# A cross-attention kernel whose inputs come laid out by columns, with column maxima for the scales and double-buffered fp16 parts

## The reference

```
q, k_t, v_t  = heads(x @ W_q), heads(text @ W_k), heads(text @ W_v)
probs_t      = softmax(q k_t^T / 4)                       # per head, 508 text tokens
text_out     = probs_t @ v_t
k_ip, v_ip   = heads(ip @ W_k_ip), heads(ip @ W_v_ip)     # 4 image tokens
qsem         = l2norm(probs_t @ text)                     # per head, 512 features
sem          = qsem @ l2norm(ip)^T
probs_ip     = softmax(q k_ip^T / 4 + 0.5 * sem) * spatial_mask
out          = (text_out + probs_ip @ v_ip) @ W_out + b_out + x
```

## Time and profile before

| | us |
|---|---|
| median of the runs | 1828.28 (1827.54 to 1833.78, 3 runs) |
| the profiled execution, as timed | 1832.93 |
| its span, first to last instruction | 1831.2 |
| busy over the span: PE, DVE, ACT, POOL | 1742.6, 1244.5, 1184.2, 1231.0 |
| first product of the first stage | at 31.94 |
| last mirror transpose of the first stage ends | at 336.78 |
| first exponential of the second stage | at 357.98 |
| first unit | at 371.65 |

### The profile page before, as it was taken

One profiled execution on the slowest core, in us unless ns is written; L12 is line 12 of the kernel. 1 busy time (PEld: TensorE's weight loads), 2 busy tenths in 40 slices (PEclk: granted clock), 3 DMA queues, 4 the chain that ended last, 5 costly groups with the idle time before them and its releaser, 6 DMA issues.

```text
span 1831.2 us, 48590 instructions
## 1 busy us (share of the span) xinstructions
PE 1742.6 (95%) x14421; PEld 1106.2 (60%) x14421; DVE 1244.5 (68%) x2872; ACT 1184.2 (65%) x2644; POOL 1231.0 (67%) x1414
## 2 busy tenths in 40 slices
PE   4999999499999999999999999999999999999899
PEld 2767766356666566666566666656566666666455
DVE  5445454267777677777677777767677777777684
ACT  3444555367777677777677777767677777777321
POOL 3122112278888788888788888878788888888310
PEclk8899999799999999999999999999999999999999
DMA  5354553736777777765665686666657656854133
GB/s 160 109 144 134 137 171 106 142 72 91 91 100 112 89 93 100 113 91 91 104 91 89 101 117 92 101 93 102 86 85 115 91 89 100 99 90 77 38 101 100
DMA packets 427592, 187.95 MB, mean 103 GB/s; under 512 B 384728, under 2 KB 415072, under 8 KB 427392
## 3 DMA queue, kind: packets, MB, share of 16 engines
q1 hardware_dynamic: 425088, 183.40, 59.0%
q10 hardware_dynamic: 2304, 2.14, 0.4%
HBM read 67.21 MB, written 34.39 MB: 55 GB/s over the span
## 4 chain that ended last, share of the span: by engine, by line
POOL 39%; PE 27%; issue 24%; DMA 3%; DVE 3%; POOLq 2%; ACT 1%; SPq 1%; ACTq 0%; DVEq 0%
POOL probs L587 17%; POOL probs L594 17%; PE bank L1287 13%; PE bank L1495 3%; PE bank L1430 3%; POOL reduced L602 2%; POOL wkv L580 2%; PE bank L1431 2%; DMA late<-wkv 2%; PE bank L1345 2%; PE bank L1496 1%; POOL reduced L601 1%; PE bank L1395 1%; PE bank L1404 1%; DVE reduced L1018 1%
## 5 line engine op out<-in xcount | busy, mean ns | idle before, releaser
L1430 PE MATMUL bank<-u_sb,late 127*128 127x508 f16 x2560 | 946.2, 376 | 0.0
L1431 PE MATMUL bank<-u_sb,late 127*128 127x508 f16 (+3 forms) x2560 | 763.0, 298 | 0.0
L1091 DVE TENSOR_REDUCE neg_max<-bank 128x1 f32<-128x508 f32 x640 | 439.1, 686 | 368.5 <-PE bank L1395 368.4
L580 POOL TENSOR_TENSOR wkv<-probs,wkv 128x508 f16<-128x508 f32 x320 | 358.6, 1121 | 219.6 <-ACT wkv L817 219.4
L1429 PE MATMUL bank<-v_ring,late 127*128 127x41 f16 x2560 | 468.8, 183 | 12.5 <-DMA late<-wkv 8.0
L1100 DVE SCALAR_TENSOR_TENSOR probs<-bank,probs 128x508 f32<-128x508 f32 x640 | 432.5, 676 | 6.3 <-PE bank L1431 6.3
L1429 PEld LDWEIGHTS bank<-v_ring,late 127*128 127x128 f16 x2560 | 247.2, 97 | 245.6 <-DMA late<-wkv 10.7
L594 POOL TENSOR_TENSOR probs<-probs,late 128x508 f32<-128x508 f32 x320 | 368.6, 1152 | 0.0
L587 POOL TENSOR_TENSOR probs<-probs,wkv 128x508 f32<-128x508 f32 x320 | 357.6, 1118 | 0.0
L1430 PEld LDWEIGHTS bank<-u_sb,late 127*128 127x128 f16 x2560 | 248.3, 97 | 167.5 <-issue 2.4
L1395 PE MATMUL bank<-x_sb,work 96*128 96x508 bf16 x640 | 242.1, 379 | 41.7 <-DMA x_sb<-k_parts 18.5
(11 more groups left out here) (166 smaller groups left out, 1804.7 us busy)
## 6 DMA issues: line engine op xcount, KB each, us to landing
x_sb<-in_x SPq DMA_DIRECT2D x16, 640.0 KB, 5.1
reduced<-in_ctx SPq DMA_DIRECT2D x32, 256.0 KB, 5.0
work<-q_parts SPq DMA_DIRECT2D x32, 240.0 KB
x_sb<-k_parts SPq DMA_DIRECT2D x32, 238.1 KB
u_parts<-u_sb SPq DMA_DIRECT2D x8, 825.5 KB, 4.2
u_sb<-u_parts SPq DMA_DIRECT2D x8, 825.5 KB, 5.3
v_parts<-v_sb SPq DMA_DIRECT2D x8, 820.0 KB, 8.2
v_ring<-v_parts SPq DMA_DIRECT2D x32, 205.0 KB, 9.0
```

Source lines behind the costliest of these rows:

```text
L580: nc.gpsimd.tensor_tensor(rows[:, 1, :, 0:TP], probs[:, j % PROB_RING, :].rearrange("p (k t) -> p k t", k=TT), rows[:, 0, :, 0:TP], ALU.su ...
L1091: nc.vector.tensor_reduce(neg_max[:, j % 4:j % 4 + 1], bank[S_BANK + j % 2][:, 0:T], AX.X, ALU.max, negate=True)\
L1430: nc.tensor.matmul(y, hi_k, u_sb[0:TP, par, GH[k]:GH[k] + T], start=(k == 0), stop=False)
L1431: done = nc.tensor.matmul(y[:, k * TP:T], hi_k, u_sb[0:TP, par, UL[k]:UL[k] + U_COLS[k]], start=False, stop=(k == TT - 1))
```

## The change

The host hands over x and the text by columns (`x_cols`, `ctx_cols`), the image tokens apart, and the weight of Q with its last 64 rows twice. PE's 28 transposes of inputs per batch go. One ACT instruction for x and one for the text write the high parts, two and one of DVE the rest, into `x_t[par]` and `ctx_t[par]`, of which there are two now, by the parity of the batch. The inputs of the batch after the next are loaded into one raw buffer (`raw`) as soon as the next one's parts are written.

x's last 64 features: the high part lies in partitions 0 to 63 of the third tile and the rest in 64 to 127, against the weight's rows twice, so that a Q tile is 8 matmuls for 9.

A scale now comes from the largest magnitude of each column: DVE reduces, squares and adds (`column_sums`), PE spreads the sum by one product with a full matrix of ones, and each partition computes the scales itself. `column_sums` of the next batch stands after the third Q residual, the product after K, the splits between and behind the V tiles. Bank 7 is given back early; the mirror transposes move from bank 3 to bank 0, and Gram blocks and V tiles change banks.

At the start PE waits for the ones only, the Q weight and x are scaled before the other weights' sums are done, and the constants are asked for later. At the end of the first stage the first two groups of heads and the Gram parts of batch 0 are loaded between the last K store and the last V store; the Gram parts of batch 1 come after the fifth DMA transpose.

```diff
-            def load_ctx(b):
-                for k in range(TT):
-                    sp.dma_start(ctx_sb[:, k, :], ctx[b, k * TP:k * TP + P, :]).then_inc(ctx_loaded, 16)
+            def load_columns(b):
+                sp.dma_start(raw_x, x_cols[b]).then_inc(x_loaded, 16)
+                sp.dma_start(raw_ctx, ctx_cols[b]).then_inc(ctx_loaded, 16)
...
+            def columns_of(b):
+                sp.wait_ge(in_lo_split, 2 * b)
+                apart(sp)
+                load_columns(b)
+
+            def first_heads():
+                sp.wait_ge(in_lo_split, 2 * B)
+                sp.wait_ge(parts_saved, 1 + 16 * 2 * NC * (B - 1))
+                sp.wait_ge(v_saved, 1 + 16 * (B - 1))
+                sp.wait_ge(u_saved, 1 + 16 * (B - 1))
+                load_group(sp, 0, 0, 0)
+                load_values(sp, 0, 0, 0)
+                sp.dma_start(u_sb[:, 0, :], u_parts[0]).then_inc(u_loaded, 16)
+                load_group(sp, 0, 1, 1)
+                load_values(sp, 0, 1, 1)
...
+            store_batch(B - 1, first_heads)
...
+                    if first and j == 9:
+                        sp.wait_ge(u_saved, 1 + 16 * B)
+                        sp.dma_start(u_sb[:, 1, :], u_parts[1]).then_inc(u_loaded, 16)
...
+            def column_sums(b):
+                dve.wait_ge(x_loaded, 16 * (b + 1))
+                nc.vector.tensor_reduce(col_max[:, ET:IN_TILES], raw_x, AX.X, ALU.max, apply_absolute_value=True).then_inc(stat_step, 1)
+                dve.wait_ge(ctx_loaded, 16 * (b + 1))
+                nc.vector.tensor_reduce(col_max[:, 0:ET], raw_ctx, AX.X, ALU.max, apply_absolute_value=True).then_inc(stat_step, 1)
...
+            def split_x(b, par):
+                dve.wait_ge(in_hi_split, 2 * b + 1)
+                both, third = x_t[par], x_t[par][64:P, 0, NC - 1, :]
...
                 for t in range(NC):
                     residual(t)
+                if not last:
+                    column_sums(b + 1)
                 for t in range(NC, 2 * NC):
                     residual(t)
+                if not last:
+                    find_top(SCALE_JOB, b, 0, 2)
...
                     if k == 1 and not last:
-                        squares(b + 1)
+                        make_scales(b + 1, 1 - par)
+                    if k == 2 and not last:
+                        split_x(b + 1, 1 - par)
+                if not last:
+                    split_ctx(b + 1, 1 - par)
...
-        Q_JOB = [(0, 2), (1, 2), (2, 2)]
...
-        V_JOB = [(6, 2), (2, 3), (0, 3), (1, 3)]
...
-        G_JOB, GT_JOB = [(4, 3), (5, 3), (6, 3), (7, 4)], (3, 3)
...
+        Q_JOB = [(0, 1), (1, 1), (2, 1)]
+        K_JOB = [(3, 1), (4, 1), (5, 1)]
+        V_JOB = [(6, 1), (0, 2), (1, 2), (2, 2)]
+        IPS_JOB = (7, 2)
+        G_JOB, GT_JOB = [(3, 2), (4, 2), (5, 2), (6, 2)], (0, 3)
...
+                free(SCALE_JOB)
+                if last_batch:
+                    pe.sem_inc(bank_filled[SCALE_JOB[0]], 1)
+                else:
+                    pe.wait_ge(sums_ready, 2 * (b + 2))
+                    spread_sums(SCALE_JOB, 0, 2)
...
-            pe.wait_ge(u_loaded, 32)
+            pe.wait_ge(u_loaded, 16)
```

More of the change, by code:

```diff
@@ L98, in xattn_kernel @@
         ident16 = sb("ident16", [P, P], fp16)
-        ones_row = sb("ones_row", [1, P], fp32)
+        ones = sb("ones", [P, P], fp32)
         headmask = sb("headmask", [P, NC, H], fp32)
@@ L317, in xattn_kernel @@
         CTX_COL, X_COL, Q_COL, K_COL = range(4)
+        WK_COL, WV_COL, WQ_COL = range(3)
         V_DOWN, SEM_DOWN = 2.0 ** -16, 2.0 ** -13
@@ L675, in _ @@
[L675 to L680 removed]
+            weight_first(wvx, wv_raw, WV_COL)
             def ip_tokens():
@@ L689, in ip_tokens, with batch @@
                 act.wait_ge(bank_drained[1], ip_use(1))
-            def batch(b, first, last):
-                act.wait_ge(bank_drained[SCALE_JOB[0]], use(SCALE_0, 0) if first else use(SCALE_JOB, b - 1))
-                apart(act)
-                for t in range(IN_TILES):
-                    j = (XT_JOB + CT_JOB)[t]
-                    act.wait_ge(bank_filled[j[0]], use(j, b))
-                    if t < NC:
-                        cn = CT[t][1]
-                        nc.scalar.activation(x_t[0:cn, 0, t, :], bank[j[0]][0:cn, 0:S], ACT.Identity,
-                                             scale=scale[0:cn, X_COL:X_COL + 1]).then_inc(in_hi_split, 1)
-                    else:
-                        nc.scalar.activation(ctx_t[:, 0, t - NC, :], bank[j[0]][:, 0:T], ACT.Identity,
-                                             scale=scale[:, CTX_COL:CTX_COL + 1]).then_inc(in_hi_split, 1)
-                if first:
-                    weight_first(wk, wk_raw, 0)
-                    weight_first(wvx, wv_raw, 1)
+            def batch(b, par, first, last):
                 def ip_columns():
@@ L773, in batch @@
                                              scale=2.0 * GRAM_SCALE).then_inc(gram_hi2_split, 1)
-                    if k == 0 and not last:
-                        scale_root(b + 1)
                 act.wait_ge(bank_filled[GT_JOB[0]], use(GT_JOB, b))
@@ L1272, in ip_tokens, with batch @@
                     last.then_inc(bank_filled[j], 1)
-            def batch(b, first, last_batch):
+            def batch(b, par, first, last_batch):
                 def free(job):
@@ L1279, in free @@
                         pe.wait_ge(bank_drained[job[0]], count)
-                def products(out, terms):
-                    n = 0
-                    for stationary, moving in terms:
-                        for a, m in SPLIT:
-                            n += 1
-                            last = nc.tensor.matmul(out, stationary(a), moving(m), start=(n == 1), stop=(n == len(SPLIT) * len(terms)))
-                    return last
-                pe.wait_ge(x_loaded, 16 * (b + 1))
-                for j in XT_JOB:
-                    free(j)
@@ L1307, in batch, with products @@
-                if first:
-                    first_scales()
+                def products(out, terms, more=()):
+                    pairs = [(stationary(a), moving(m)) for stationary, moving in terms for a, m in SPLIT] + list(more)
+                    for n, (stationary, moving) in enumerate(pairs):
+                        last = nc.tensor.matmul(out, stationary, moving, start=(n == 0), stop=(n == len(pairs) - 1))
+                    return last
+                x_b, ctx_b = x_t[par], ctx_t[par]
```

437 lines of the change are left out of this document (193 added, 244 removed).

## The result

The kernel after takes 1854.13 us (median of 4 runs, 1845.80 to 1858.18), the one before 1827.91 (1827.33 to 1833.78): a ratio of 1.013, with a 95% interval of 1.009 to 1.017. The forecast was 1782.9, with 1769 to 1803 as its range, and a slower kernel had 3 chances in 100. The change made it **slower, by 1.3%**, some 24 us by that ratio.

A forecast was written before the change was run, and what follows sets the result against it. PE was taken to bound the first and second stages. Batches -25.9, start -11.2 and seam -8.3 sum to -45.4 us, from the median 1828.28 to 1782.9 us, range 1769 to 1803; forecast chance 0.60.

The forecast's parts named there:

- the last of the sum: Second and third stages: every instruction on PE is kept, so they contribute 0 us.
- Start: Kernel start with batch 0: first Q product at 22.1 us for 31.94; -11.2 us in all, range -9 to -16.
- One batch: First stage: without input transposes PE takes 32.7 us a batch for 36.4, -3.7 each, -25.9 over seven.
- The new wait: Ahead of each batch's Q: its first tile waits until ACT frees bank 0, +0.9 us a batch.
- rival 3: First stage: the maxima or last splits on DVE are late, 1.5 to 3 us a batch, 1793 to 1804; chance 0.13.
- rival 4: First stage: single raw buffer makes loads late, 22 us or more from issue; slower, 1850 at 24 us; chance 0.03.
- rival 5: First stage: the prefetch leaves PE waiting 5 to 6 us each batch, about 1825 us; chance 0.02.
- Rival 1: First-stage batches: the wait for bank 0 lowers PE's granted clock, +8 us, or 12 giving 1795; chance 0.12.
- Seam: Between first and second stage: earlier loads put the first unit 26.6 us behind the stage's end for 34.9; -8.3, -5 to -13.
- E: The end of the first stage, 336.8 us before the change, foretold at about 299.5 after it.

The follow-up runs named there:

- ACT's return to its old place: Kernel after with 94 empty instructions on ACT ahead of its wait for the saved parts: 1826.64 us, ratio to the kernel before 0.998.
- DVE's residence: Kernel after with 94 empty instructions on ACT and 64 on DVE ahead of its first row maximum: 1809.04 us, ratio 0.986.
- ACT's residence: Kernel after with 34 empty instructions on ACT and 64 on DVE, the version with both loops resident: 1791.00 us, ratio 0.980.
- ACT's 34: Kernel before with 34 empty instructions on ACT, its second-stage loop starting where it does after the change: 1874.98 us, ratio 1.025.
- the two without it: Kernel after, ACT +34 and DVE +64, first-stage Q and V banks turned: 1789.59 us; the same with 105 empty instructions on PE: 1780.65 us.

## Why the prediction was wrong

**The step that failed** is the last of the sum: "The second and third stages keep every instruction on PE: 0." It is true of the instructions, and false of the time. I had shown that PE bounds the stage and looked for a changed instruction on it; there was none. The stage loops, though, and a loop's cost depends on where its code lies, which everything ahead of it moves. It was worth +59.7 us in the profiles. By the stage's length in them ACT's return to its old place gives back 36.5 (1379.2 to 1342.7), DVE's residence 7.5 (to 1335.2) and ACT's residence 16.6 (to 1318.6). Each of these is one execution; by the ratios to the kernel before, times 1828, the same three steps give 28, 22 and 11 us. So the sum of some 60 is shown and the shares are known to about 10 us. The mechanism by which a place costs time, instructions fetched anew at a round's start, is supported by the packets and by the pauses that hold them; what makes one place resident and another not stays open.

A part of the loss is the clock: of the 59.7 us PE's idle time is 49, and in the other 10.6 PE is busy for longer with the same instructions. The profile of the kernel after has seven stretches inside the stage in which the granted clock is 0.50 for 3.4 us or more, the one before three, and the kernel before with ACT's 34 twelve. One of the seven, in the columns of the earlier trace rows:

```profile
1213.20:1216.60 3.40, 3.40 (x15) 1.44 (x16) 1.89 (x4) 0.68 (x1) 2.19 (x4) 0.50 0.50 82
```

Each costs about half its length, so the four more are some 7 us, an estimate from these lengths. The third stage was as forecast.

The text said that a second stage longer by more than 5 us would be wrong and that it had no mechanism for it. The mechanism could be seen ahead: the row of 107 instruction packets in the profile of before, the idle 2.1 us at each round's start that the profile puts down to DVE, and a diff that writes a body out twice.

**The rest held**, and with both loops resident the span is 1788.2 us where the sum foretold 1785.8.

- *Start.* First Q at 22.84, foretold 22.1. The V weight's squares ended at 17.7, not 16.9. The reduces took 1.75 and 2.27 us, foretold 1.8 and 2.3. The Trainium skill ("VectorE: DVE Perf Modes", Rules for kernel authors) calls the reduce the slowest DVE operation; over 2032 fp32 columns this trace has 2.27 us for it and 2.32 for the multiply-subtract, so here it isn't:

```profile
9.79 2.27 DVE L905 TENSOR_REDUCE col_max<-raw 128x4 f32<-128x2032 f32 x1
...
23.29 2.32 DVE L938 SCALAR_TENSOR_TENSOR reduced<-raw,scale,reduced 128x2032 f16<-128x2032 f32 x1
```

- *One batch.* 32.58 us, foretold 32.7. The new wait measured 1.02 (0.9), put down to ACT's copy at L781, the ones product started without a wait, and Q took 5.83. DVE was never late: rivals 3, 4 and 5 did not come. Loads of x and context landed in 4.5 and 7.6 us, so the single raw buffer did not bind.
- *Clock.* Rival 1 came in part. Four of the six periods between batches were 34.2 instead of 32.6 (a mean clock of 0.95 in the first row above), and the last was 36.6, foretold as any other: it has a wait of 0.68 ahead of the image scores, and its Gram block runs 8.80 us for 6.74. The stage ended at 306.9, foretold 299.5; this is the second miss of the sum, 7 us. With the same first stage, other profiles had none to six long periods and began its last mirror transposes between 296.4 and 309.8 (306.3 here), so a part of this is the execution's own. Over seven profiles with the 1.0 us wait 24 of 42 periods were long, over the two without it 2 of 12. That speaks for rival 1's mechanism and doesn't prove it.
- *Seam.* First exponential at E + 18.1, foretold 17; first unit at E + 27.3, foretold 26.6. ACT waited for the last store of Gram parts until 323.67, E + 16.8 (foretold 16).

## What to carry to other kernels

A loop on an engine is not free of what stands ahead of it. Where a change adds or removes instructions ahead of a hot loop, compare the instruction queue's packets and the idle time ahead of the loop's first instruction before and after; if they moved, place the loop with empty instructions at a point where the engine waits anyway, and try several places, as the built program's count didn't give the good one here. A comparison of two versions that leaves this out measures their places as well: here it hid a gain of 37 us in the start, the batches and the seam under a loss of 60 in the stage behind them.

Price the stages that a change doesn't touch not at zero, but at what a shift of their loops could do.

## What the hardware showed unasked

- 34 empty instructions on one engine, executed once during a wait, made the kernel 2.5% slower; 34 on ACT and 64 on DVE made the other version 3% faster.
- ACT's loop of 349 instructions was refetched at four of the five places tried, with an idle time ahead of a round of 2.1 to 2.6 us in seven kernels and 4.5 to 5.0 in three, and stayed resident at one, with 0.1 to 0.3 in four.
- An increment of a semaphore took PE 0.15 us: 189 of them filled the 28.4 us between two scores. The 94 on ACT were hidden in its wait of 16 us: the first unit still came 27.2 us behind the first stage's end.
